# In the second attention VectorE opens each piece of the 4-bit codes at the end of the preceding step

## The chip, the cores and the metric

One core of a Trainium2 chip runs the whole program. The metric is device time in microseconds (us) from one launch to its end, the median over runs. The program holds two transformer layers; the change touches one stage of it, the second attention, in which TensorE (PE), VectorE (DVE), ScalarE (ACT), GpSimd (POOL) and the DMA queue of SyncE (SP) work side by side.

## The reference, cut to what matters

```python
# 4 x 256 tokens, width 512
x = layernorm(x + L0_attention(x)); x = layernorm(x + L0_gptq_ffn(x))
x = layernorm(x + L1_attention(x))          # 32 heads, 8 key heads, two causal attentions
x = layernorm(x + L1_nf4_ffn(x))
...
# in L1_nf4_ffn, for each of three weight matrices:
flat = w.reshape(-1, 64)
absmax = max(abs(flat), axis=1)
normalized = flat / where(absmax == 0, 1, absmax)
idx = searchsorted(bounds, normalized)      # 15 bounds, 16 codes
w = NF4_CODE[idx] * absmax
```

The code lookup is written as a sum of 15 steps: a first value plus, for every bound, a jump where `normalized` is at or above that bound. It depends on weights alone, so the kernel does it during the second attention and leaves the finished weights in DRAM for the last feed-forward block.

## The kernel before, in words

The second attention runs in 8 groups of 4 heads. A group has 16 steps (4 batches by 4 heads; each step handles two attentions of one head). `groups` (L1125) writes group 0 out, runs groups 1 to 6 as a loop of the engines (`Fori`), and writes group 7 out; so each engine takes the loop's branch back five times. No planner orders the work: each engine's order is the order of its own code, and semaphores tie the engines.

In step n VectorE does, in this order: `peaks(n)` (L1640, two reductions over the scores in PSUM, for which ScalarE's exponentials wait), `codes(n)`, `shares(n)` (L1646, reciprocals of the sums), `probs_low(n-1, 0)` (L1651, the low half of the turned probabilities of the first attention), `out_low(n-2)` (L1656), the rotation of one projected unit (L1619 to L1625), `probs_low(n-1, 1)` (L1651 again), in every fourth step `add_output` (L1664), and the step's remaining units, most of them the low half of a value unit (L1629, "the values") and in some steps a key unit (L1619 to L1625 at 256 columns).

ScalarE does in step n: `exps(n)` (L1348), `out_high(n-2)` (L1373), `probs_high(n-1, 0)` (L1367), `shares_applied(n)` (L1357), `code_terms(n)` (L1384, L1390), `probs_high(n-1, 1)` (L1367), then the high halves of the units (L1334, L1338). TensorE does `scores(n)`, a projection, `apply(n-2)`, `turn(n-1, 0)`, `output(n-3)`, `turn(n-1, 1)` (L1519, which waits for the first `probs_low`), then the remaining projections. GpSimd does in step n: splits of loaded weight pieces (L1260, L1262), the sums of the code terms (L1290), and the low half of the rotated unit (L1271), which the scores two steps later need.

The codes: a group handles 4 pieces of weights, 128 x 512 (the fourth 128 x 576). Each has 15 terms, spread over steps by `CODE_STEP`: the pieces begin in steps 0, 5, 8 and 11. About half of the terms of a step are VectorE's (L1710), the others ScalarE's, and GpSimd adds them up. A piece is opened by `code_start` on VectorE, four instructions: L1685 (largest magnitude by block of 64), L1688 and L1691 (its inverse, 8 or 9 columns), L1693 (the piece times the inverse, into `nf_unit`, which all terms read), each behind a wait for the one before; the last line is a wait of VectorE's queue for L1693 itself. A piece is closed by `code_end` (L1673, in place on the sum), which waits for GpSimd's last sum. In the kernel before, both stand in `codes(n)` of the piece's first step, behind `peaks(n)`: first `code_end` of the old piece, then `code_start` of the new one, then the first terms. SP's queue loads the next piece after `nf_unit_done` and stores a piece after `code_end`.

Of the kernel before, what the change touches and what calls it, by code (L numbers as in the profile page):

```python
# [22 lines left out]
GROUPS, PER = 8, 4  # L23
# [8 lines left out]
STEPS = PER * BATCH  # L32
# [973 lines left out]
def l1_units(first, last):  # L1006
# [7 lines left out]
CODE_AT = (0, 8 * BLK, 16 * BLK, 24 * BLK, 33 * BLK)  # L1014
CODE_STEP = [0] * 3 + [1] * 3 + [2] * 3 + [3] * 3 + [4] * 3 + [5] * 5 + [6] * 5 + [7] * 5 + [8] * 5 + [9] * 5 + [10] * 5 \
    + [11] * 3 + [12] * 2 + [13] * 2 + [14] * 4 + [15] * 4
CODE_RING = 5
STEEP = 2.0 ** 60

# [37 lines left out]
def l1_attention_block(nc, X, XT, LQ, signals, norm, normed, ident, banks, w_ql, w_vk, w_o, w_nf, coded_w, early):  # L1057

    NP = 2
    with ExitStack() as ctx:  # L1060
# [16 lines left out]
        nf_raw, nf_unit = sb("nf_raw", [P, LARGEST], F32), sb("nf_unit", [P, LARGEST], F32)  # L1077
        nf_acc, nf_term = sb("nf_acc", [P, CODE_AT[1] + LARGEST], F32), sb("nf_term", [P, CODE_RING, LARGEST], F32)
        lq_first = early["lq_w"]
# [82 lines left out]
        def code_slot_free(g, first, i):  # L1162

            if first and i < CODE_RING:
                return 0
            q, k = divmod(i - CODE_RING, 15)
            return 14 * (PER * g + q) + max(k, 1)

        def acc_cell(q, n):
            return nf_acc[:, q % 2 * CODE_AT[1]:q % 2 * CODE_AT[1] + n]  # L1170

        def code_cols(q):
            return CODE_AT[q], CODE_AT[q + 1] - CODE_AT[q]
# [59 lines left out]
        def _(pool):  # L1233
            def body(g, first, last):
# [39 lines left out]
                def code_sums(n):  # L1274

                    for i, step in enumerate(CODE_STEP):
# [6 lines left out]
                        acc = acc_cell(q, w)  # L1283
                        left = nf_term[:, (i - 1) % CODE_RING, 0:w] if k == 1 else acc
                        held = [(nf_terms_act, terms_made(g, i + 1, True)), (nf_terms, terms_made(g, i + 1, False)),
# [3 lines left out]
                        hold(pool, passed["pool"], *held)  # L1289
                        pool.tensor_tensor(acc, left, nf_term[:, i % CODE_RING, 0:w], ALU.add).then_inc(nf_added, 1)  # L1290

# [301 lines left out]
        def _(dve):  # L1593
# [10 lines left out]
            def body(g, first, last):  # L1604
                number, place = span("units", first, last, g)
                roped, roped_place = span("roped", first, last, g)
                plain, _ = span("plain", first, last, g)
# [24 lines left out]
                def unit_low(name):  # L1632
                    plain_low(name) if name[0] == "VL" else rotate(name)
# [33 lines left out]
                def code_end(q):  # L1667

                    _, n = code_cols(q % PER)
                    cell = acc_cell(q, n).rearrange("p (a c) -> p a c", c=BLK)  # L1670
                    wide = nf_top[:, q % 2, 0:n // BLK].unsqueeze(2).to_broadcast([P, n // BLK, BLK])
                    dve.wait_ge(nf_added, 14 * (PER * g + q + 1))
                    dve.scalar_tensor_tensor(out=cell, in0=cell, scalar=-1.0, in1=wide, op0=ALU.add, op1=ALU.mult)\  # L1673
                       .then_inc(nf_coded, 1)

                def code_start(q):

                    _, n = code_cols(q)
                    piece, m = PER * g + q, n // BLK
                    cut = lambda x: x[:, 0:n].rearrange("p (a c) -> p a c", c=BLK)  # L1680
                    top = nf_top[:, q % 2, 0:m]
                    dve.wait_ge(nf_landed, 16 * (piece + 1))
                    if not (first and q == 0):
                        dve.wait_ge(nf_terms_act, terms_made(g, 15 * q, True))
                    dve.tensor_reduce(top, cut(nf_raw), mybir.AxisListType.X, ALU.max, apply_absolute_value=True,  # L1685
                                      negate=True).then_inc(nf_measured, 1)
                    dve.wait_ge(nf_measured, 3 * piece + 1)
                    dve.scalar_tensor_tensor(out=nf_safe[:, 0:m], in0=top, scalar=0.0, in1=top, op0=ALU.is_equal,  # L1688
                                             op1=ALU.add).then_inc(nf_measured, 1)
                    dve.wait_ge(nf_measured, 3 * piece + 2)  # L1690
                    dve.reciprocal(nf_inv[:, 0:m], nf_safe[:, 0:m]).then_inc(nf_measured, 1)  # L1691
                    dve.wait_ge(nf_measured, 3 * piece + 3)
                    dve.tensor_tensor(cut(nf_unit), cut(nf_raw), nf_inv[:, 0:m].unsqueeze(2).to_broadcast([P, m, BLK]),  # L1693
                                      ALU.mult).then_inc(nf_unit_done, 1)
                    dve.wait_ge(nf_unit_done, piece + 1)

                def codes(n):
                    for q in range(PER):
                        ended = CODE_STEP[15 * q - 1] + 1 if q else 0
                        if ended == n and not (first and q == 0):  # L1700
                            code_end(q - 1)
                    for i, step in enumerate(CODE_STEP):
                        q, k = divmod(i, 15)
                        if step != n or CODE_ACT[i]:
                            continue
                        _, w = code_cols(q)
                        if k == 0:
                            code_start(q)
                        wait(dve, nf_added, code_slot_free(g, first, i))
                        dve.tensor_scalar(nf_term[:, i % CODE_RING, 0:w], nf_unit[:, 0:w], -BOUNDS[k], JUMPS[k],  # L1710
                                          ALU.is_ge, ALU.mult).then_inc(nf_terms, 1)
# [4 lines left out]
                for n in range(STEPS):  # L1716
                    peaks(n)
                    if first and n == 0:
                        normalise(dve, X, norm, 1, 1, late)
                    codes(n)  # L1720
                    shares(n)
                    if not (first and n < 1):
                        probs_low(n - 1, 0)
                    if not (first and n < 2):
                        out_low(n - 2)
                    units = l1_step_units(n, last)
                    for name in units[0:1]:
                        unit_low(name)
                    if not (first and n < 1):
                        probs_low(n - 1, 1)  # L1730
                    if n % PER == 2 and not (first and n < 3):
                        add_output(n - 3)
                        if last and n > PER:
                            tiles = range(2 * (n // PER) - 2, 2 * (n // PER))
                            dve.wait_ge(out_free, 2 * (BATCH * g + n // PER))
                            measure(dve, X, norm, normed, tiles)
                    for name in units[1:]:
                        unit_low(name)
                    if first and n < 2:
                        for i in range(2):  # L1740
                            low_tile(dve, XT, OUT[i], signals, 2, TT // 2 + 2 * n + i)
                    if first and n == 2:
                        lq_low(1, OUT[0])
# [558 lines left out]
```

## Time and profile before

| | |
|---|---|
| median of 3 runs | 2422.95 us (2421.2 to 2423.99) |
| profiled execution, its own time | 2422.93 us |
| its span | 2421.1 us, granted TensorE clock 0.971 |
| PE busy | 2239.8 us (93%) |
| DVE busy | 1804.6 us (75%) |
| ACT busy | 1433.2 us (59%) |
| POOL busy | 1577.2 us (65%) |
| second attention | about 786 to 2195 us of the span |

A row of the timeline is: start in us from the span's start, duration in us, engine, line, operation, tile written and tiles read (names as the program has them; tiles that share a buffer go by one name, so `q_packed` also stands for several small tiles, `q_hot` for the high halves of the probabilities), shapes, count of merged instructions, and in brackets the idle time of the engine before it with what ended it. A row with x2 or x3 merges back-to-back instructions. "issue" as a releaser means that the engine waited for nothing that the profile shows.

### The profile page before, as it was taken

To read this page: it belongs to the slowest core of one execution; us is meant where nothing else is said; L and a number is where in the kernel's file an instruction comes from. 1 tells how busy PE (TensorE), PEld (TensorE's weight loads), DVE (VectorE), ACT (ScalarE), POOL (GpSimd) and SP (SyncE) were. 2 spreads that over 40 slices of the span, in tenths; PEclk is the share of its full clock that TensorE was granted. 3 is DMA by queue.
4 is the path that set the end of the run, shared out by engine and by line. 5 is a ranking of instruction groups with operands and counts; after the bars stand their busy time and mean duration, and the time that the engine had idled before them with its cause. 6 is when DMAs were issued, how large, how long until landed. Compare 5 with 4: busy or idle time off the path is not lost. (4 is left out here: it accounts for less than half of the span.)

```text
span 2421.1 us, 43785 instructions
## 1 busy us (share of the span) xinstructions
PE 2239.8 (93%) x14144; PEld 1987.9 (82%) x14144; DVE 1804.6 (75%) x3266; ACT 1433.2 (59%) x3949; POOL 1577.2 (65%) x1340
## 2 busy tenths in 40 slices
PE   6899999988999899999999999999999999987998
PEld 5788888876888788888888888888888888876886
DVE  5788777767633898888888888888888888964332
ACT  2657766653233676676666666676676766663232
POOL 3656657413364678878878878788788788642343
PEclk8999999988999999999999999999999999988999
DMA  3201111000000101101101111111111111004000
GB/s 102 63 24 46 58 34 44 11 2 26 19 25 25 47 15 56 55 20 55 48 26 58 39 39 50 39 45 43 40 46 47 31 50 41 19 5 148 1 18 18
DMA packets 49556, 95.39 MB, mean 39 GB/s; under 512 B 6768, under 2 KB 14224, under 8 KB 48976
## 3 DMA queue, kind: packets, MB, share of 16 engines
q1 hardware_dynamic: 49296, 92.24, 12.2%
q8 instruction: 125, 2.05, 0.4%
q14 instruction: 135, 1.11, 0.1%
HBM read 81.47 MB, written 10.75 MB: 38 GB/s over the span
## 5 line engine op out<-in xcount | busy, mean ns | idle before, releaser
L1290 POOL TENSOR_TENSOR a_nf_acc<-a_nf_acc,a_nf_term 128x512 f32<-128x512 f32 (+1 forms) x416 | 588.9, 1416 | 145.4 <-ACT a_nf_term L1390 76.7
L1348 ACT ACTIVATE a_probs<-bank,q_packed 128x128 f32<-128x128 f32 (+1 forms) x512 | 208.4, 419 | 193.4 <-DVE q_packed L1640 193.4
L1357 ACT ACTIVATE a_probs<-a_probs,q_packed 128x128 f32<-128x128 f32 (+1 forms) x512 | 192.5, 463 | 68.9 <-DVE q_packed L1646 68.9
L1848 POOL TENSOR_TENSOR f_w_lo<-WGU,f_w_hi 128x512 fp32r<-128x512 f32 x88 | 112.4, 1295 | 175.5 <-ACT f_w_hi L1891 175.5
L1271 POOL TENSOR_TENSOR a_qk_lo<-q_packed,a_qk_hi 128x512 fp32r<-128x512 f32 (+1 forms) x160 | 193.7, 1212 | 44.5 <-ACT a_qk_hi L1334 44.5
L64 PE MATMUL bank<-a_wo_hi,a_ot_hi 128*128 128x512 f32 x512 | 212.5, 415 | 0.0
L1651 DVE TENSOR_TENSOR e_pt_lo<-bank,q_hot 128x384 fp32r<-128x384 f32 x256 | 141.0, 551 | 91.2 <-ACT q_hot L1367 90.4
L1710 DVE TENSOR_SCALAR a_nf_term<-a_nf_unit 128x512 f32<-128x512 f32 (+1 forms) x288 | 200.1, 740 | 3.4 <-DVE a_nf_unit L1693 0.9
L66 PE MATMUL bank<-a_wo_hi,a_ot_lo 128*128 128x512 f32 x512 | 201.4, 393 | 0.0
L65 PE MATMUL bank<-a_wo_lo,a_ot_hi 128*128 128x512 f32 x512 | 201.1, 393 | 0.0
L1334 ACT ACTIVATE a_qk_hi<-q_packed 128x512 fp32r<-128x512 f32 (+1 forms) x160 | 94.3, 590 | 176.0 <-DVE q_packed L1625 176.0
L480 ACT ACTIVATE a_probs<-bank,a_dip 128x128 f32<-128x128 f32 (+1 forms) x256 | 104.1, 419 | 139.5 <-DVE a_dip L903 139.5
L1519 PE MATMUL bank<-ident,a_probs 128*128 128x128 f32 x768 | 134.0, 284 | 56.5 <-DVE e_pt_lo L1651 56.5
L64 PE MATMUL bank<-q_hot,XT_hi 128*128 128x320 f32 x512 | 171.5, 335 | 6.9 <-DVE a_crossed L1622 6.9
L400 POOL TENSOR_TENSOR a_straight<-a_straight,a_crossed 128x512 f32<-128x512 f32 x64 | 82.1, 1283 | 132.2 <-DVE a_crossed L886 132.2
L1625 DVE TENSOR_TENSOR q_packed<-q_packed,a_crossed 128x512 f32<-128x512 f32 (+1 forms) x160 | 156.5, 978 | 5.5
L65 PE MATMUL bank<-q_table,XT_hi 128*128 128x320 f32 x512 | 160.2, 313 | 0.0
L1519 PEld LDWEIGHTS bank<-ident,a_probs 128*128 128x128 f32 x768 | 85.7, 142 | 90.7 <-DVE e_pt_lo L1651 82.2
L66 PE MATMUL bank<-q_hot,XT_lo 128*128 128x320 f32 x512 | 160.0, 313 | 0.0
L2028 DVE TENSOR_TENSOR f_hidden<-bank,f_act_gate 128x512 f32<-128x512 f32 x44 | 30.5, 692 | 165.9 <-PE bank L66 132.3
L64 PE MATMUL bank<-q_hot,a_vl_hi 128*128 128x256 f32 (+1 forms) x512 | 138.1, 270 | 9.0 <-DVE e_pt_lo L1651 8.4
L64 PE MATMUL bank<-XT_hi,f_w_hi 128*128 128x512 f32 x352 | 142.3, 404 | 3.2 <-POOL f_w_lo L1848 3.2
(244 smaller groups left out, 8461.1 us busy)
## 6 DMA issues: line engine op xcount, KB each, us to landing
q_packed<-in_l_o SPq DMA_DIRECT2D x64, 256.0 KB, 2.8
q_packed<-in_l_vk SPq DMA_DIRECT2D x32, 384.0 KB, 3.1
q_packed<-in_l_ql SPq DMA_DIRECT2D x32, 320.0 KB, 2.9
a_raw<-in_l_ou SPq DMA_DIRECT2D x32, 288.0 KB, 2.8
a_raw<-in_l_nr SPq DMA_DIRECT2D x16, 384.0 KB, 3.0
a_nf_raw<-in_w_nf SPq DMA_DIRECT2D x24, 256.0 KB, 2.6
coded_w<-a_nf_acc SPq DMA_DIRECT2D x24, 256.0 KB, 2.0
f_codes<-coded_w SPq DMA_DIRECT2D x6, 512.0 KB, 3.8
```

The source lines that it names most:

```text
L64: pe.matmul(out, lh, rh, start=first, stop=False)
L65: pe.matmul(out, lh, rl, start=False, stop=False)
L66: return pe.matmul(out, ll, rh, start=False, stop=last)
L1271: pool.tensor_tensor(rope_cell(name, QK.lo), src, rope_cell(name, QK.hi).bitcast(F32), ALU.subtract)\
L1290: pool.tensor_tensor(acc, left, nf_term[:, i % CODE_RING, 0:w], ALU.add).then_inc(nf_added, 1)
L1348: act.activation(probs[:, n % 2, col:col + keys], bank[:, at:at + keys], ACT.Exp, bias=dip[:, n % 2, i:i + 1], accum_out=total[:, n % 2, i ...
L1357: ins = act.activation(cell, cell, ACT.Copy, scale=share[:, n % 2, i:i + 1])
L1519: last_ = pe.transpose(TURN[:, i * P:(i + 1) * P], probs[:, n % 2, col:col + P], ident[:, :])
L1625: dve.tensor_tensor(row, row, crossed[:, 0:n], ALU.add).then_inc(rope_sum, 1)
L1651: dve.tensor_tensor(pt_lo_cell[:, at], TURN[:, 0:3 * P], pt_hi_cell[:, at].bitcast(F32), ALU.subtract)\
L1710: dve.tensor_scalar(nf_term[:, i % CODE_RING, 0:w], nf_unit[:, 0:w], -BOUNDS[k], JUMPS[k], ALU.is_ge, ALU.mult).then_inc(nf_terms, 1)
L1848: pool.tensor_tensor(lo, src, hi.bitcast(F32), ALU.subtract).then_inc(part_lo[i], 1)
```

## The change

`code_start` leaves `codes(n)`. A new function `next_code(n)` is called on VectorE at the end of step n, behind the remaining units. At the ends of steps 4, 7 and 10 it opens the group's second, third and fourth piece, and at the end of step 15 the first piece of the next group (except in the last group); only the very first piece is still opened in `codes(0)`. `code_end` stays in `codes` of steps 0, 5, 8 and 11, behind `peaks`. The instructions are the same ones, in another order on one engine; the other engines' code is unchanged. In `code_start` the piece's size is now taken modulo 4, as its number may be 4.

```diff
+CODE_STARTS = CODE_STEP[::15]
...
                 def code_start(q):
 
-                    _, n = code_cols(q)
+                    _, n = code_cols(q % PER)
...
+                def next_code(n):
+                    if n + 1 in CODE_STARTS:
+                        code_start(CODE_STARTS.index(n + 1))
+                    elif n == STEPS - 1 and not last:
+                        code_start(PER)
+
                 def codes(n):
-                    for q in range(PER):
-                        ended = CODE_STEP[15 * q - 1] + 1 if q else 0
-                        if ended == n and not (first and q == 0):
-                            code_end(q - 1)
+                    if n in CODE_STARTS and not (first and n == 0):
+                        code_end(CODE_STARTS.index(n) - 1)
                     for i, step in enumerate(CODE_STEP):
                         q, k = divmod(i, 15)
                         if step != n or CODE_ACT[i]:
                             continue
                         _, w = code_cols(q)
-                        if k == 0:
-                            code_start(q)
+                        if first and i == 0:
+                            code_start(0)
...
                     for name in units[1:]:
                         unit_low(name)
+                    next_code(n)
```

## Rows read from the trace of the kernel before

**Rows 1.** Waits of PE and DVE, 790 to 2196 us: total us, times, longest.
```profile
PE bank L1519 <- DVE e_pt_lo L1651: 56.5, 46, 4.9
DVE q_packed L1640 <- issue: 12.9, 5, 2.9
DVE q_packed L1640 <- PE bank L1508: 3.0, 9, 0.3
```

**Rows 2.** DVE timeline, step 6 of group 4, which opens no piece.
```profile
1549.49 1.01 DVE L1640 TENSOR_REDUCE q_packed<-bank 128x2 f32<-128x256 f32 x2
...
1553.15 0.56 DVE L1651 TENSOR_TENSOR e_pt_lo<-bank,q_hot 128x384 fp32r<-128x384 f32 x1 [0.69 <-ACT q_hot L1367]
...
1557.35 0.56 DVE L1651 TENSOR_TENSOR e_pt_lo<-bank,q_hot 128x384 fp32r<-128x384 f32 x1 [0.31 <-ACT q_hot L1367]
```

**Rows 3.** DVE timeline, step 5 of group 4, which opens the second piece.
```profile
1535.60 1.01 DVE L1640 TENSOR_REDUCE q_packed<-bank 128x2 f32<-128x256 f32 x2
1536.82 1.75 DVE L1673 SCALAR_TENSOR_TENSOR a_nf_acc<-a_nf_acc,q_packed 128x512 f32<-128x512 f32 x1 [0.21 <-POOL a_nf_acc L1290]
1538.49 0.68 DVE L1685 TENSOR_REDUCE q_packed<-a_nf_raw 128x8 f32<-128x512 f32 x1
...
1540.46 1.10 DVE L1710 TENSOR_SCALAR a_nf_term<-a_nf_unit 128x512 f32<-128x512 f32 x3
...
1541.57 0.53 DVE L1651 TENSOR_TENSOR e_pt_lo<-bank,q_hot 128x384 fp32r<-128x384 f32 x1
...
1546.04 0.56 DVE L1651 TENSOR_TENSOR e_pt_lo<-bank,q_hot 128x384 fp32r<-128x384 f32 x1 [0.63 <-ACT q_hot L1367]
```

**Rows 4.** POOL timeline of the same stretch.
```profile
1535.50 1.29 POOL L1290 TENSOR_TENSOR a_nf_acc<-a_nf_acc,a_nf_term 128x512 f32<-128x512 f32 x1 [0.18 <-POOL a_nf_acc L1290]
1536.75 1.27 POOL L1271 TENSOR_TENSOR a_qk_lo<-q_packed,a_qk_hi 128x512 fp32r<-128x512 f32 x1
```

**Rows 5.** Timelines of DVE and POOL, step 11 of group 4.
```profile
1604.43 1.56 DVE L1688 SCALAR_TENSOR_TENSOR q_packed<-q_packed 128x9 f32<-128x9 f32 x1
```
```profile
1604.40 1.56 POOL L1262 TENSOR_TENSOR a_wql_lo<-q_packed,a_wql_hi 128x640 fp32r<-128x640 f32 x1
```

**Rows 6.** Two lines of the source: count, shortest/median/longest ns, first and last start.
```profile
L1625 DVE TENSOR_TENSOR q_packed<-q_packed,a_crossed x160: 424/742/1857, 776.3 to 2153.2; 128x512 f32<-128x512 f32 x128, 128x256 f32<-128x256 f32 x32
```
```profile
L1693 DVE TENSOR_TENSOR a_nf_unit<-a_nf_raw,q_packed x32: 691/694/760, 791.0 to 2128.4; 128x512 f32<-128x512 f32 x24, 128x576 f32<-128x576 f32 x8
```

**Rows 7.** DVE and POOL timelines, step 8 of group 4, which opens the third piece.
```profile
1568.53 1.01 DVE L1640 TENSOR_REDUCE q_packed<-bank 128x2 f32<-128x256 f32 x2
...
1574.36 0.53 DVE L1651 TENSOR_TENSOR e_pt_lo<-bank,q_hot 128x384 fp32r<-128x384 f32 x1
```
```profile
1569.54 1.28 POOL L1271 TENSOR_TENSOR a_qk_lo<-q_packed,a_qk_hi 128x512 fp32r<-128x512 f32 x1
```

**Rows 8.** DVE timeline, step 11 of group 4, which opens the fourth piece.
```profile
1602.08 1.01 DVE L1640 TENSOR_REDUCE q_packed<-bank 128x2 f32<-128x256 f32 x2
...
1607.99 0.53 DVE L1651 TENSOR_TENSOR e_pt_lo<-bank,q_hot 128x384 fp32r<-128x384 f32 x1
```

**Rows 9.** DVE and POOL timelines where the loop branches back, groups 3 to 4.
```profile
1481.98 0.49 DVE L1629 TENSOR_TENSOR a_vl_lo<-bank,a_vl_hi 128x320 fp32r<-128x320 f32 x1 [0.56 <-ACT a_vl_hi L1338]
1485.02 1.02 DVE L1640 TENSOR_REDUCE q_packed<-bank 128x2 f32<-128x256 f32 x2 [2.55 <-issue]
...
1489.98 0.53 DVE L1651 TENSOR_TENSOR e_pt_lo<-bank,q_hot 128x384 fp32r<-128x384 f32 x1
```
```profile
1484.03 1.42 POOL L1290 TENSOR_TENSOR a_nf_acc<-a_nf_acc,a_nf_term 128x576 f32<-128x576 f32 x1 [0.18 <-POOL a_nf_acc L1290]
```

**Rows 10.** DVE timeline, step 0 of group 1, entered without a branch.
```profile
965.16 1.83 DVE L1673 SCALAR_TENSOR_TENSOR a_nf_acc<-a_nf_acc,q_packed 128x576 f32<-128x576 f32 x1 [2.06 <-POOL a_nf_acc L1290]
...
969.68 0.53 DVE L1651 TENSOR_TENSOR e_pt_lo<-bank,q_hot 128x384 fp32r<-128x384 f32 x1
```

**Rows 11.** DVE timeline, step 11 of group 7: L1673 at its shortest.
```profile
2126.60 0.68 DVE L1673 SCALAR_TENSOR_TENSOR a_nf_acc<-a_nf_acc,q_packed 128x512 f32<-128x512 f32 x1
```

## The prediction

> **What bounds the kernel now.** I read the waits of the second attention first, then the timelines of VectorE, GpSimd and ScalarE step by step, since the change only reorders one engine inside that stage.
>
> TensorE is the busiest engine, but it doesn't set the pace of this stage: it is the one that waits, 56.5 us in 46 places, for the low half of the first probabilities (L1651) [rows 1]. VectorE, in contrast, finds the scores ready when it comes to `peaks`: over 128 steps it waited 3.0 us in nine of them for PE, and 12.9 us in five for "issue" [rows 1]. So the pace is a ring of VectorE and ScalarE: peaks, then exponentials, `out_high` and `probs_high` on ScalarE, then `probs_low` on VectorE, and so on to the next peaks. An addition to this ring moves everything behind it, PE too.
>
> A step without an opening shows the ring at its fastest. From the start of peaks to the first L1651 it takes 1553.15 - 1549.49 = 3.66 us, and before that L1651 VectorE sat idle for ScalarE; from there to the second L1651 4.20 us, idle for ScalarE again [rows 2]. In a step that opens a piece VectorE is the late one: 1541.57 - 1535.60 = 5.97 us to the first L1651, with no idle before it, and 4.47 to the second, 10.44 in all [rows 3]. That is the stall the change aims at.
>
> **The change part by part.** Nothing is added or removed: four instructions and their waits go from behind peaks and `code_end` to ahead of peaks. The added waits of the queue are satisfied when reached: ScalarE made the terms of step n before `probs_high(n-1, 1)`, which VectorE has already waited for, and the load of the piece was issued a whole piece ago. SP's loads of the next piece are released some us earlier, its stores by `code_end` somewhat later; neither was late, cost nothing. ScalarE's terms aren't released earlier, as they stand behind `shares_applied`. GpSimd's first sum waits for VectorE's first two terms, which stay behind `code_end`.
>
> What moves is peaks. Call S the time from the opening's first instruction to peaks. After the change the first L1651 comes S + 3.66 after the end of the previous step, for the remaining work between (peaks 1.01, `code_end` 0.68 when undisturbed, three terms 1.10 [rows 3, 11]) is about 2.8 us and fits into ScalarE's 3.66. The second comes 4.20 later.
>
> How long is S? Alone, the opening takes 1540.46 - 1538.49 = 1.97 us [rows 3]. That is the lower end. But there it ran while GpSimd had nothing to do. At the end of a step GpSimd is adding terms and then makes the low half of the rotated unit: 1535.50 to 1536.79 and 1536.75 to 1538.02 [rows 4]. Some VectorE instructions don't run beside a GpSimd one: L1673 took 1.75 instead of 0.68 us [rows 3, 11] and ended 0.55 after GpSimd's instruction did [rows 3, 4]; L1688, a matter of 0.17 us, took 1.56 beside L1262, begun 0.03 earlier [rows 5]; L1625 goes from 424 to 1857 ns [rows 6]. L1693 was never longer than 760 [rows 6], but neither did it ever stand beside GpSimd work; it is the same operation as L1625, on two tiles in SBUF. I take it as held likewise. The upper end is then both L1688 and L1693 held for a whole GpSimd instruction of about 1.3 us: S = 4.5.
>
> The Trainium skill ("SBUF — State Buffer", section "SBUF: two separate sides") says that a VectorE instruction with two SBUF inputs and a GpSimd one that reads SBUF exclude each other, for the whole length of whichever began first. The rows of L1673 and L1688 agree; for L1693 no row here shows it, and the rule speaks for the held S, thus against this change. Without it one would take 1.97 for every opening.
>
> Step 5, worked through: L1685 runs 1535.60 to 1536.28; L1688 asks at 1536.31 and gets through when the sum ends at 1536.79; L1691 follows; L1693 asks at 1537.14 and must wait for GpSimd's L1271, now ending at 1538.06; it ends 0.55 later, at 1538.61; peaks start at 1538.70. S = 3.10. First L1651: 6.76 against 5.97. Second: 10.96 against 10.44, **+0.52**. The gain is real (the hold of L1673 and its 0.21 wait for GpSimd go, worth 1.28, since L1673 now runs when GpSimd is idle) but smaller than what replaces it: 1.13 of holds, and ScalarE's 3.66, no longer hidden under the opening.
>
> Step 8: GpSimd's L1271 ends at 1570.82 [rows 7], so L1693 ends near 1571.4 and S = 2.97; first L1651 at 6.63 against 5.83; second at 10.83 against 5.83 + 4.47 = 10.30: **+0.53**.
>
> Step 11: 5.91 us now [rows 8]; S lies between 2.1 (576 columns, not held) and 3.1. GpSimd works through L1271 and then the splits there, the place in the sequence is open, so I take 2.5: 6.16, **+0.25**.
>
> The loop's back edge, five times: here VectorE is idle 2.55 us ahead of peaks with nothing to wait for [rows 9]; five such places make the 12.9 us [rows 1]. It looks like a hole which the opening could fill. I don't think it does: the hole is the branch, and the branch stands behind `code_start`'s last line, the wait for L1693. So the sequence becomes opening, then branch, then peaks. L1685 from 1482.40; L1688 through at 1483.85, when a sum ends; L1693 held by the next sum (1484.03 to 1485.45) until 1486.04; then the branch. Between the start of the values' last instruction and peaks there are 1485.02 - 1481.98 = 3.04 us, between its end and peaks 2.55 [rows 9]; behind a wait I take 2.9. Peaks at 1488.95, first L1651 at 1492.61 instead of 1489.98: **+2.63** (2.3 to 2.8 by the two ends).
>
> The Trainium skill ("Runtime: NRT & Kernel Launch", section "Instruction fetch mechanics") says that a taken branch to a target outside the fetched window stalls until the page has come. The five idle stretches, one for each back edge, agree. By it nothing behind the branch can start earlier than the branch allows, and the opening's closing wait delays the branch.
>
> The two entries without a branch (groups 1 and 7): now 7.59 us from peaks (965.16 - 2.06 - 1.01 = 962.09) to 969.68, because `code_end` waited 2.06 for GpSimd and was held for 1.83 [rows 10]. After: held by two sums of 1.43 us, S = 3.9, plus 3.66 = 7.56: **0**.
>
> In group 7 step 11 L1673 isn't held now [rows 11], so the saving of 1.07 is missing from the balance: **+1.07**.
>
> Sum: 8 groups x (0.52 + 0.53 + 0.25) = 10.4; 5 x 2.63 = 13.2; 1.07; together +24.7 us. PE takes this over in full: its stall at `turn` grows by the same amounts, and it has no backlog to catch up with, since VectorE hardly ever waits for it. The profiled execution took 2422.93 us (span 2421.1 and 1.8 around it), the same as the median of 2422.95. 2422.9 + 24.7 = **2448 us**.
>
> **The rivals.**
>
> A. *The openings aren't held* (L1693 runs beside GpSimd, and L1688 slips through). Place: ends of steps 4, 7, 10, 15. For it: L1693's row has no long case. Against: L1625. With S = 1.97: step 5 9.83 against 10.44, -0.61; step 8 -0.47; step 11 -0.13: 8 x -1.21 = -9.7; back edge 1482.40 + 1.9 + 2.9 + 3.66 = 1490.9, +0.9 each, 4.6; the two entries, bound by GpSimd's sums, -1.8 each, -3.6; group 7 +1.1. Sum -7.6: **2415 us**, faster. It decides from a mean hold of 7.6 / 31 = 0.25 us for a moved opening; the forecast has about 1.0.
>
> B. *The branch hides the opening*, held as forecast: peaks at the back edge come when L1693 is done, 1486.1, first L1651 at 1489.8, -0.2 each. 10.4 + 1.1 - 1.0 = +10.5: **2433 us**. For it: the hole is there. Against: the wait ahead of the branch.
>
> C. *A and B together*: peaks at the back edge stay at 1485.02, first L1651 at 3.66 instead of 4.96, -1.3 each. -9.7 - 6.5 - 3.6 + 1.1 = -18.7: **2404 us**.
>
> D. *Holds and stalls are longer than forecast*: GpSimd gets through ahead of the waiting L1688 in a third of the 31 moved openings, 10 x 1.3 = 13, with PE's longer stalls costing it some clock: **2460 us**.
>
> E. *PE has slack that takes the additions up*, if its work had a reserve behind the stalls: the forecast is cut to under 5 us, **2426 us**. For it: in nine steps VectorE did wait for PE [rows 1]. Against it stands that PE waits for the same L1651 and moves along.
>
> **How the numbers follow.** Forecast 0.68, A 0.06, B 0.12, C 0.03, D 0.08, E 0.03. Range: B and the forecast and part of D: 2430 to 2457 us; A, C, E and the far part of D, under 2 in 10, are left out. The likeliest's own range is 2442 to 2453. A measurement of this kernel tells 0.2%, 4.8 us, from no change. Faster: A and C, 0.09. Same: E and a bit, 0.04. Slower 0.87.
>
> **What would show it.** L1693 at about 1.3 to 1.5 us in the changed trace where it was 0.69, and L1688 above 0.17 in several places; L1673 at 0.68 in steps 5 and 8. 6.6 to 6.8 us from the end of the values to the first L1651 in steps 5 and 8, with idle for ScalarE before it. At the back edge an idle stretch of 2.5 to 3.0 us behind L1693 and not before L1685, and PE's stall there some 2.6 us longer. PE's total wait for L1651 up from 56.5 to some 80. The prediction is wrong if L1693 stays at 0.69 (rival A) or if peaks follow L1693 without a hole at the back edge (rival B).

## The result, and the profile after

The changed kernel takes 2455.67 us (median of four runs, 2453.15 to 2458.24) against 2422.07 us of the kernel before beside it (four runs, 2421.1 to 2423.99): +33.6 us, ratio 1.0138 with a 95% interval of 1.0126 to 1.0151. The forecast was 2448 us, +25, with a range up to 2457. The sign and the mechanism hold; the size was short by about 9 us. The result also lies above the 2442 to 2453 us that the prediction gave its own case, and nearer to rival D's 2460 than to 2448.

In the changed kernel's listing the lines have moved: peaks L1641, the first-row reciprocal L1647, `probs_low` L1652, the rotation's last instruction L1626, `code_end` L1674, the opening L1686, L1689, L1692 and L1694, VectorE's terms L1715, GpSimd's sums L1291 and its low halves L1272.

From the page of the changed kernel, the engines' busy time and two groups of instructions (busy us, mean ns of one, idle before them and who ended it):

```profile
PE 2250.9 (92%) x14144; PEld 2001.4 (81%) x14144; DVE 1818.1 (74%) x3266; ACT 1429.9 (58%) x3949; POOL 1581.5 (64%) x1340
...
L1349 ACT ACTIVATE a_probs<-bank,q_packed 128x128 f32<-128x128 f32 (+1 forms) x512 | 208.8, 420 | 287.2 <-DVE q_packed L1641 287.2
...
L1358 ACT ACTIVATE a_probs<-a_probs,q_packed 128x128 f32<-128x128 f32 (+1 forms) x512 | 192.7, 469 | 6.8 <-DVE q_packed L1647 6.8
```

ScalarE's wait for the reciprocal (68.9 us before) is almost gone, because VectorE no longer comes to it late; its wait for peaks has grown from 193.4 to 287.2 us. What the change moved is in these two figures: VectorE is late for the first link of the ring instead of a later one. The waits of the changed kernel, 790 to 2232 us (total, times, longest), answer to [rows 1]:

```profile
PE bank L1520 <- DVE e_pt_lo L1652: 84.1, 47, 5.1
DVE q_packed L1641 <- issue: 15.7, 5, 3.3
DVE q_packed L1641 <- PE bank L1509: 1.9, 5, 0.8
```

TensorE waits 84.1 us for the first probabilities instead of 56.5, and the five idle stretches ahead of peaks are still there, and longer. VectorE at the end of step 4 and in step 5 of group 4, against [rows 3]:

```profile
1554.75 0.68 DVE L1686 TENSOR_REDUCE q_packed<-a_nf_raw 128x8 f32<-128x512 f32 x1
1555.46 0.51 DVE L1689 SCALAR_TENSOR_TENSOR q_packed<-q_packed 128x8 f32<-128x8 f32 x1
...
1556.24 1.49 DVE L1694 TENSOR_TENSOR a_nf_unit<-a_nf_raw,q_packed 128x512 f32<-128x512 f32 x1
1557.85 1.02 DVE L1641 TENSOR_REDUCE q_packed<-bank 128x2 f32<-128x256 f32 x2
1558.79 0.68 DVE L1674 SCALAR_TENSOR_TENSOR a_nf_acc<-a_nf_acc,q_packed 128x512 f32<-128x512 f32 x1
1559.39 1.09 DVE L1715 TENSOR_SCALAR a_nf_term<-a_nf_unit 128x512 f32<-128x512 f32 x3
...
1561.53 0.56 DVE L1652 TENSOR_TENSOR e_pt_lo<-bank,q_hot 128x384 fp32r<-128x384 f32 x1 [0.69 <-ACT q_hot L1368]
...
1565.72 0.56 DVE L1652 TENSOR_TENSOR e_pt_lo<-bank,q_hot 128x384 fp32r<-128x384 f32 x1 [0.31 <-ACT q_hot L1368]
...
1568.30 1.27 DVE L1626 TENSOR_TENSOR q_packed<-q_packed,a_crossed 128x256 f32<-128x256 f32 x1
1569.49 1.01 DVE L1641 TENSOR_REDUCE q_packed<-bank 128x2 f32<-128x256 f32 x2
```

GpSimd beside it:

```profile
1554.65 1.29 POOL L1291 TENSOR_TENSOR a_nf_acc<-a_nf_acc,a_nf_term 128x512 f32<-128x512 f32 x1 [0.18 <-POOL a_nf_acc L1291]
1555.90 1.28 POOL L1272 TENSOR_TENSOR a_qk_lo<-q_packed,a_qk_hi 128x512 fp32r<-128x512 f32 x1
...
1567.99 1.29 POOL L1272 TENSOR_TENSOR a_qk_lo<-q_packed,a_qk_hi 128x512 fp32r<-128x512 f32 x1
```

L1689 gets through when GpSimd's sum ends (1555.94), L1694 is held by the low half that begins at 1555.90 and ends 0.55 us after it (1557.73 against 1557.18). "Held" means here: the row is longer than the instruction takes alone, because it ends only after a GpSimd instruction that began before it. From L1686 to peaks are 1557.85 - 1554.75 = 3.10 us, and from peaks to the first L1652 3.68, with an idle for ScalarE in it. These are the forecast's 3.10 and 3.66.

The back edge, groups 4 to 5, VectorE, GpSimd and TensorE of the changed kernel:

```profile
1676.33 0.49 DVE L1630 TENSOR_TENSOR a_vl_lo<-bank,a_vl_hi 128x320 fp32r<-128x320 f32 x1 [0.56 <-ACT a_vl_hi L1339]
...
1677.44 0.79 DVE L1689 SCALAR_TENSOR_TENSOR q_packed<-q_packed 128x8 f32<-128x8 f32 x1
...
1678.50 1.85 DVE L1694 TENSOR_TENSOR a_nf_unit<-a_nf_raw,q_packed 128x512 f32<-128x512 f32 x1
1683.39 1.02 DVE L1641 TENSOR_REDUCE q_packed<-bank 128x2 f32<-128x256 f32 x2 [3.04 <-issue]
...
1687.06 0.56 DVE L1652 TENSOR_TENSOR e_pt_lo<-bank,q_hot 128x384 fp32r<-128x384 f32 x1 [0.69 <-ACT q_hot L1368]
```
```profile
1678.38 1.42 POOL L1291 TENSOR_TENSOR a_nf_acc<-a_nf_acc,a_nf_term 128x576 f32<-128x576 f32 x1 [0.18 <-POOL a_nf_acc L1291]
```
```profile
1687.68 0.90 PE L1520 MATMUL bank<-ident,a_probs 128*128 128x128 f32 x3 [4.84 <-DVE e_pt_lo L1652]
```

and the same place of TensorE in the kernel before:

```profile
1663.86 0.55 PE L1519 MATMUL bank<-ident,a_probs 128*128 128x128 f32 x3 [2.05 <-DVE e_pt_lo L1651]
```

The opening ends at 1680.35, and only then do three idle microseconds begin: the branch stands behind it. TensorE's stall is 2.79 us longer.

**Where the 33.6 us lie.** The starts of peaks, taken from both traces for all 128 steps, give the added time by place (changed minus before, us). 36.1 us come between the first and the last peaks; ahead of the stage and behind it the two profiled executions differ by -0.8. (The profiled execution of the changed kernel is the longest of its four, 2.6 us above the median, so this column adds up to more than 33.6.) The last column is the same difference for the pair e8 and e9 below.

| place | forecast | measured | e9 - e8 |
|---|---|---|---|
| steps 4 and 5, eight times | 4.2 | 7.1 | 4.3 |
| steps 6 to 9, eight times | 4.2 | 7.9 | 6.1 |
| steps 10 to 14, eight times | 3.1 | 0.8 | 0.9 |
| step 15 to step 3 over a back edge, five times | 13.2 | 18.3 | 21.6 |
| the same over the two entries | 0 | 1.9 | 0.1 |

### The profile page after: what moved, and what is told of

Same layout as the page of the kernel before. It is cut to its first block and busy times, and to the rows that moved or that the text cites. A ratio compares the mean times of both kernels' runs of the same rounds, so it can differ in the third digit from the quotient of the medians.

```text
span 2456.4 us, 43784 instructions
## 1 busy us (share of the span) xinstructions
PE 2250.9 (92%) x14144; PEld 2001.4 (81%) x14144; DVE 1818.1 (74%) x3266; ACT 1429.9 (58%) x3949; POOL 1581.5 (64%) x1340
## 3 DMA queue, kind: packets, MB, share of 16 engines
q8 instruction: 125, 2.05, 0.4%
## 5 line engine op out<-in xcount | busy, mean ns | idle before, releaser
L1291 POOL TENSOR_TENSOR a_nf_acc<-a_nf_acc,a_nf_term 128x512 f32<-128x512 f32 (+1 forms) x416 | 589.7, 1418 | 172.0 <-ACT a_nf_term L1391 108.5
L1349 ACT ACTIVATE a_probs<-bank,q_packed 128x128 f32<-128x128 f32 (+1 forms) x512 | 208.8, 420 | 287.2 <-DVE q_packed L1641 287.2
L1272 POOL TENSOR_TENSOR a_qk_lo<-q_packed,a_qk_hi 128x512 fp32r<-128x512 f32 (+1 forms) x160 | 198.2, 1240 | 56.9 <-ACT a_qk_hi L1335 56.9
L1652 DVE TENSOR_TENSOR e_pt_lo<-bank,q_hot 128x384 fp32r<-128x384 f32 x256 | 141.7, 553 | 109.5 <-ACT q_hot L1368 108.7
L1520 PE MATMUL bank<-ident,a_probs 128*128 128x128 f32 x768 | 136.3, 288 | 84.2 <-DVE e_pt_lo L1652 84.1
L1715 DVE TENSOR_SCALAR a_nf_term<-a_nf_unit 128x512 f32<-128x512 f32 (+1 forms) x288 | 202.2, 746 | 0.0
L1626 DVE TENSOR_TENSOR q_packed<-q_packed,a_crossed 128x512 f32<-128x512 f32 (+1 forms) x160 | 162.6, 1016 | 5.5
L1641 DVE TENSOR_REDUCE q_packed<-bank 128x2 f32<-128x256 f32 (+1 forms) x256 | 129.7, 547 | 20.5 <-issue 15.7
```

The source lines that it names most:

```text
L1272: pool.tensor_tensor(rope_cell(name, QK.lo), src, rope_cell(name, QK.hi).bitcast(F32), ALU.subtract)\
L1349: act.activation(probs[:, n % 2, col:col + keys], bank[:, at:at + keys], ACT.Exp, bias=dip[:, n % 2, i:i + 1], accum_out=total[:, n % 2, i ...
L1520: last_ = pe.transpose(TURN[:, i * P:(i + 1) * P], probs[:, n % 2, col:col + P], ident[:, :])
L1626: dve.tensor_tensor(row, row, crossed[:, 0:n], ALU.add).then_inc(rope_sum, 1)
L1641: ins = dve.tensor_reduce(dip[:, n % 2, 2 * r:2 * r + 2], scores, mybir.AxisListType.X, ALU.max, negate=True)
L1652: dve.tensor_tensor(pt_lo_cell[:, at], TURN[:, 0:3 * P], pt_hi_cell[:, at].bitcast(F32), ALU.subtract)\
```

## The experiments

Each kernel is compared with runs of the kernel before beside it on the same chip; their median was 2421.96 us for e1, e2, e3 and e6, 2422.01 for e4, e5 and e7, and 2421.39 for e8 and e9.

**e1: only the openings inside a group are moved.**

```
-                    elif n == STEPS - 1 and not last:
-                        code_start(PER)
...
-                        if first and i == 0:
+                        if i == 0:
                             code_start(0)
```

> Only the openings of the second to fourth piece are moved (ends of steps 4, 7, 10); a group's first piece is opened in step 0 as in the kernel before. My theory (ring of VectorE and ScalarE, openings held by GpSimd's instructions): +11 us by the sums of the prediction (8 x 1.3 + 1.1), +15 us with what the changed trace adds to the steps behind an opening (about 1.9 us in a group); 2434 to 2438 us. If the openings were not held: about -8 us, 2414 us. If only the loop's back edge costs anything: 0, 2422 us.

**e2: only the opening over the group's end is moved.**

```
-                    if n + 1 in CODE_STARTS:
-                        code_start(CODE_STARTS.index(n + 1))
-                    elif n == STEPS - 1 and not last:
+                    if n == STEPS - 1 and not last:
                         code_start(PER)
...
-                        if first and i == 0:
-                            code_start(0)
+                        if k == 0 and (q > 0 or first):
+                            code_start(q)
```

> Only the opening of the next group's first piece is moved (end of step 15); the others stay behind peaks and code_end. My theory (the loop's branch stands behind the opening's closing wait, and the opening is held): +13 us by the prediction, +18 us by the changed trace (5 x 3.2 at the back edges, 2 at the two entries without a branch); 2436 to 2441 us. If the branch's idle time hid the opening: -1 us, 2421 us. If this and the run with the inner openings are independent, the two differences add up to that of the whole change (+33.6 us).

Measured: e1 2440.15 us (ratio 1.0076, 1.0059 to 1.0093), +18.2; e2 2439.23 (1.0072, 1.0055 to 1.0089), +17.3. Together 35.5, near the 33.6 of the whole. So each half does its own harm, and the two add. Both are dearer than the forecast's terms, 11.5 and 13.2 us, and e1 lies above the 2434 to 2438 us expected of it.

**e3: the opening's closing wait stands ahead of the first term, so that the branch is not behind it.**

```
                                       ALU.mult).then_inc(nf_unit_done, 1)
-                    dve.wait_ge(nf_unit_done, piece + 1)
...
+                        if k == 0:
+                            dve.wait_ge(nf_unit_done, PER * g + q + 1)
```

> The whole change, but the last line of the opening, VectorE's wait for its own L1694, stands ahead of the piece's first term instead of at the opening's end. My theory: the branch can now be taken while L1694 is still held, so peaks at the five back edges come some 1.8 us earlier (L1694 took 1.85 us there), -9 us, and peaks after the other openings 0.1 to 0.2 us earlier, -3 us: about 2444 us, and the idle stretch between L1694 and peaks at the back edge shrinks from 3.0 to about 1.2 us. If the closing wait has no part in it (the branch is late for another reason): 2456 us, idle stretch unchanged at 3.0.

Measured: 2441.1 us (1.0076, 1.0059 to 1.0093), 14.6 below the changed kernel. VectorE's wait ahead of peaks, and TensorE's stall at the same back edge, in its trace:

```profile
DVE q_packed L1641 <- issue: 6.0, 5, 1.4
```
```profile
1680.27 0.90 PE L1520 MATMUL bank<-ident,a_probs 128*128 128x128 f32 x3 [3.01 <-DVE e_pt_lo L1652]
```

L1694 there still takes 1.84 us, but the idle behind it falls from 15.7 us in all to 6.0. So the branch does run beside the held instruction once nothing ahead of it waits for that instruction's end. Of the 18.3 us at the back edges 6.9 are left, and 9.7 of the 11.4 saved are this idle time: the wait in front of the branch, and not the opening itself, is most of that loss. It is rival B's mechanism, bought with one line; in the change as made it wasn't there.

**e6: the opening behind peaks, but ahead of `code_end`.**

```
-                    if n in CODE_STARTS and not (first and n == 0):
-                        code_end(CODE_STARTS.index(n) - 1)
+                    if n in CODE_STARTS:
+                        code_start(CODE_STARTS.index(n))
+                        if not (first and n == 0):
+                            code_end(CODE_STARTS.index(n) - 1)
...
-                    next_code(n)
```

> Each piece is opened in its first step as in the kernel before, behind peaks, but ahead of code_end instead of behind it. My theory: peaks stay early, so ScalarE's exponentials run beside the opening; the opening fills VectorE's wait for GpSimd's last sum, and only L1689 is held, by L1272, after which code_end runs free (0.68 us). First L1651 in steps 5 and 8 about 5.3 us behind the start of peaks instead of 5.97 and 5.83, at the back edge 4.4 instead of 5.0: 8 x 1.55 + 5 x 0.55 + 1.8 = -17 us, 2405 us. If the order of the same VectorE instructions behind peaks made no difference (the length of VectorE's work is what counts): 2422 us.

Measured: **2402.39 us** (ratio 0.9922, 0.9905 to 0.9938), 19.6 us below the kernel before and 53 below the changed one. It beats both. VectorE in its step 5 of group 4:

```profile
1525.81 1.01 DVE L1641 TENSOR_REDUCE q_packed<-bank 128x2 f32<-128x256 f32 x2
1526.74 0.68 DVE L1686 TENSOR_REDUCE q_packed<-a_nf_raw 128x8 f32<-128x512 f32 x1
1527.45 0.83 DVE L1689 SCALAR_TENSOR_TENSOR q_packed<-q_packed 128x8 f32<-128x8 f32 x1
...
1528.55 0.69 DVE L1694 TENSOR_TENSOR a_nf_unit<-a_nf_raw,q_packed 128x512 f32<-128x512 f32 x1
1529.38 0.69 DVE L1674 SCALAR_TENSOR_TENSOR a_nf_acc<-a_nf_acc,q_packed 128x512 f32<-128x512 f32 x1
...
1531.08 0.53 DVE L1652 TENSOR_TENSOR e_pt_lo<-bank,q_hot 128x384 fp32r<-128x384 f32 x1
```

The reduction L1686 takes its usual 0.68 beside GpSimd's low half (which runs from 1526.96), L1689 is held for 0.66, and by then GpSimd is done: L1694 and `code_end` run free. From peaks to the first L1652 are 5.27 us instead of 5.97 [rows 3]. It removes `code_end`'s hold, which the change aimed at, without putting anything ahead of peaks.

**e7: the opening right behind peaks, `code_end` at the end of the same step.**

```
-                    if n in CODE_STARTS and not (first and n == 0):
-                        code_end(CODE_STARTS.index(n) - 1)
+                    if n in CODE_STARTS:
+                        code_start(CODE_STARTS.index(n))
...
-                    next_code(n)
+                    if n in CODE_STARTS and not (first and n == 0):
+                        code_end(CODE_STARTS.index(n) - 1)
```

> Each piece is opened in its first step right behind peaks, and the old piece's code_end goes to the end of that step, behind the values, where the change had put the opening. My theory: the first L1651 comes 4.6 us behind the start of peaks in steps 5 and 8, but code_end then stands in the ring at the step's end, held by GpSimd's sums (0.7 to 1.9 us): gain of the one and loss of the other nearly cancel against the variant with the opening ahead of code_end: 2405 to 2418 us, 2411 us as the middle. If whatever stands at a step's end is free: 2400 us or less.

Measured: 2410.98 us (0.995, 0.9933 to 0.9966). The first L1652 comes 4.65 us behind peaks in step 5, earlier than in e6, but `code_end` at the end of the step is held in its turn (1.29 us in step 8, 1.59 in step 0) and stands ahead of the next peaks. So the end of a step is a bad place for `code_end` as well.

**e4 and e5: the kernels before and after, with GpSimd's sums in steps 4, 7, 10 and 15 cut to the first 64 columns (the other columns of these sums are left out).**

```
-                        pool.tensor_tensor(acc, left, nf_term[:, i % CODE_RING, 0:w], ALU.add).then_inc(nf_added, 1)
+                        w = BLK if n in (4, 7, 10, 15) else w
+                        pool.tensor_tensor(acc[:, 0:w], left[:, 0:w], nf_term[:, i % CODE_RING, 0:w], ALU.add)\
+                            .then_inc(nf_added, 1)
```

> The kernel before, in which GpSimd's sums of code terms in steps 4, 7, 10 and 15 cover only the first 64 of 512 or 576 columns; the other columns' additions are left out. So GpSimd is quiet at the ends of these steps. It is the control for the same cut in the changed kernel. My theory (VectorE's two-input instructions are held by GpSimd's): code_end is no longer held (saves 1.07, and its wait for the last sum), nor are L1625 and L1710 around it: -25 to -40 us, 2382 to 2397 us. If GpSimd's work were off VectorE's path: -2 us at most.

> The changed kernel with the same cut: GpSimd's sums in steps 4, 7, 10 and 15 cover only the first 64 columns; the other columns' additions are left out. My theory: the openings run free or nearly so, S falls from 3.1 to 2.0-2.2 us, L1694 takes 0.69 us again at the ends of steps 4 and 7; the whole falls by about 33 us or more from the changed kernel, to about 2415 to 2425 us, yet stays some 20 us slower than the control with the same cut, because peaks still stand behind the opening and the branch behind its wait. If the holds were the whole cause: equal to the control within 5 us. If they were no cause: the gap to the control stays at 33 us and L1694 at 1.5 us.

Measured: e4 2378.73 us (0.9827, 0.9811 to 0.9844), just below the 2382 to 2397 expected, and e5 2418.9 (0.9988, 0.9978 to 0.9997). L1694's counterpart in e5 (count; shortest/median/longest ns):

```profile
L1696 DVE TENSOR_TENSOR a_nf_unit<-a_nf_raw,q_packed x32: 691/693/759, 794.2 to 2125.8; 128x512 f32<-128x512 f32 x24, 128x576 f32<-128x576 f32 x8
```

against the changed kernel's:

```profile
L1694 DVE TENSOR_TENSOR a_nf_unit<-a_nf_raw,q_packed x32: 693/1485/1861, 791.2 to 2162.5; 128x512 f32<-128x512 f32 x24, 128x576 f32<-128x576 f32 x8
```

The hold of L1694 is gone from every opening, and the opening takes 1.96 us at steps 4 and 7. That shows GpSimd's work to be the cause of the hold. (In step 10 a short one is left: L1689's counterpart takes 0.99 us.) But the distance between the pair is 40.2 us and not about 20: I had expected the holds to be half of the loss, and this expectation fell. The control shows why. With GpSimd quiet at the step's end, `code_end` behind peaks isn't held either in steps 5 and 8 (0.68), and the first `probs_low` of step 5 comes at 4.60 us instead of 5.97. Against a ring of 3.68 there are then 0.92 us to gain, and an unheld opening of 1.96 ahead of peaks costs 1.04 (the two traces give 8.5 us for the eight places of steps 4 and 5, 1.06 each). A place's price is the opening's length less what the first `probs_low` can still gain down to ScalarE's 3.7 us. Holds enter both terms.

**e8 and e9: the kernels before and after, with GpSimd's sums of steps 0, 5 and 9 (from a piece's third term on) cut to 64 columns in the same way (the rest of those sums is left out).**

```
+                        w = BLK if n in (0, 5, 9) and k > 1 else w
```

> The kernel before, with GpSimd's sums of steps 0, 5 and 9 (from the third term of a piece on) cut to the first 64 columns; the other columns of these sums are left out. It is the control of the next run. Cutting takes short-lived GpSimd work from 64 of the places in which VectorE's step behind the openings can be held, so the control itself is 5 to 15 us faster than the kernel before: 2407 to 2417 us.

> The changed kernel with the same cut. The forecast was right up to the value it was worked out for (second probabilities of the step in steps 5 and 8, first ones at the back edge), and the changed kernel lost some 9 us more than forecast. Theory: those 9 us are instructions of VectorE further on (rotated units and terms of steps 0, 5 and 9), which now meet one of GpSimd's sums. Then this kernel is 22 to 29 us slower than its control, near the forecast's 24.7. Rival: the 9 us lie elsewhere (TensorE's longer stalls, its clock); then the distance to the control stays at 32 to 36 us, as it was between the two kernels in full.

Measured: e8 2407.83 us (0.9946, 0.9932 to 0.9959), e9 2444.77 (1.0092, 1.0076 to 1.0107): 36.9 us apart and not 22 to 29. So what GpSimd's sums hold isn't the whole of the missing 9 us. By place (the table's last column) it is a part: steps 4 and 5 drop from 7.1 to 4.3 us, which is the forecast's 4.2, and steps 6 to 9 from 7.9 to 6.1. At the back edges the loss grows instead, from 18.3 to 21.6. Where VectorE had been held, it now waits for TensorE, in step 1 of group 5 of e9:

```profile
1687.36 1.02 DVE L1643 TENSOR_REDUCE q_packed<-bank 128x2 f32<-128x256 f32 x2 [0.65 <-PE bank L1511]
...
1691.50 0.56 DVE L1654 TENSOR_TENSOR e_pt_lo<-bank,q_hot 128x384 fp32r<-128x384 f32 x1 [1.16 <-ACT q_hot L1370]
```

Stretches of e9 behind its stall of 4.96 us (the stretch, its length, busy us and instructions of PE, PE's weight loads, DVE, ACT and POOL, then the granted clock, and the DMA engines' share and GB/s):

```profile
1682.00:1684.00 2.00, 2.00 (x10) 2.00 (x9) 1.97 (x4) 1.97 (x4) 0.06 (x1) 0.50 0.03 11
1684.00:1686.00 2.00, 2.00 (x10) 2.00 (x9) 1.30 (x3) 0.96 (x3) 0.65 (x2) 0.50 0.04 8
```

TensorE runs at 0.50 of its clock, the 1.2 GHz level, through some 4 us of solid work, and the next scores come late.

## Why the prediction came out as it did

**What bounds the stage: right.** The ring of VectorE and ScalarE sets the pace. The two halves of the change, moved alone, add up, and in steps 0, 5, 8 and 11 of the groups above the first `probs_low` follows peaks by 3.68 us, ScalarE's chain.

**The length S of the opening: right.** Forecast 3.10, 2.97, 2.5 us, 3.9 for the entries. Peaks of steps 5, 8 and 11 came 3.10, 2.97 and 2.52 us later in the middle groups, those behind the entries 3.82. L1694 was held by GpSimd as L1625 had been, which no row of the kernel before showed; the Trainium skill ("SBUF — State Buffer", section "SBUF: two separate sides") had it so, and L1694's median of 1.49 us agrees, as does its 0.69 in e5 where GpSimd is brief.

**The gain from `code_end`: right.** 0.68 us in steps 5 and 8 where it took 1.75; no wait for GpSimd's last sum ahead of it.

**Up to the second `probs_low` of steps 5 and 8: right.** 3.10 + 7.87 = 10.97 us forecast 10.96, and 2.96 + 7.87 = 10.83 forecast 10.83. At the back edge the first `probs_low` is 1687.06 - 1676.33 = 10.73 us behind the start of the values' last instruction, and was 1489.98 - 1481.98 = 8.00 [rows 9]: +2.73, forecast +2.63.

**The branch behind the opening: right, and a little dearer.** The five idle stretches make 15.7 us, 3.14 each, where I had taken 2.9. The cause I gave, the closing wait ahead of the branch, is shown by e3. Over the five back edges the first `probs_low` comes 14.2 us later instead of 13.2.

**What failed: the tacit step that nothing changes behind the point to which a place was worked out.** "The second comes 4.20 later", and with it each place was closed, the back edges even at the first `probs_low`. This put at nothing what comes behind.

First and largest, VectorE meets other GpSimd instructions in the rest of the step. In step 5 L1626 takes 1.27 us, as it now asks 0.31 us behind the start of a low half (1568.30, 1567.99); before it asked later and paid 0.95. The same rows of the kernel before, VectorE and GpSimd:

```profile
1548.61 0.95 DVE L1625 TENSOR_TENSOR q_packed<-q_packed,a_crossed 128x256 f32<-128x256 f32 x1
```
```profile
1547.99 1.29 POOL L1271 TENSOR_TENSOR a_qk_lo<-q_packed,a_qk_hi 128x512 fp32r<-128x512 f32 x1
```

That is +0.32, on top of the forecast +0.52: 0.84 of the measured 0.89 a place. In step 9 the terms are held, VectorE and GpSimd of the changed kernel

```profile
1601.54 3.28 DVE L1715 TENSOR_SCALAR a_nf_term<-a_nf_unit 128x512 f32<-128x512 f32 x3
...
1604.83 0.52 DVE L1652 TENSOR_TENSOR e_pt_lo<-bank,q_hot 128x384 fp32r<-128x384 f32 x1
```
```profile
1601.62 1.48 POOL L1272 TENSOR_TENSOR a_qk_lo<-q_packed,a_qk_hi 128x512 fp32r<-128x512 f32 x1
1603.06 1.48 POOL L1291 TENSOR_TENSOR a_nf_acc<-a_nf_acc,a_nf_term 128x512 f32<-128x512 f32 x1
```

and in the kernel before

```profile
1581.01 2.03 DVE L1710 TENSOR_SCALAR a_nf_term<-a_nf_unit 128x512 f32<-128x512 f32 x3
```

Three terms meet two GpSimd instructions in a row and last 3.28 us instead of 2.03; the first `probs_low` comes at 4.22 us and no longer at 3.67. Both are borne out by e8 and e9 for steps 4 to 9, where cutting the sums took off 2.8 and 1.8 us of the surplus.

Behind a back edge it is the rotation's last instruction. VectorE and GpSimd in step 0 of group 5 of the changed kernel, and VectorE of the kernel before:

```profile
1690.25 1.59 DVE L1626 TENSOR_TENSOR q_packed<-q_packed,a_crossed 128x512 f32<-128x512 f32 x1
```
```profile
1690.02 1.28 POOL L1291 TENSOR_TENSOR a_nf_acc<-a_nf_acc,a_nf_term 128x512 f32<-128x512 f32 x1 [2.66 <-ACT a_nf_term L1391]
```
```profile
1666.44 0.69 DVE L1625 TENSOR_TENSOR q_packed<-q_packed,a_crossed 128x512 f32<-128x512 f32 x1
```

Because the opening is gone from behind peaks, L1626 now asks 0.23 us after a sum has begun. From the first `probs_low` to the second it takes 4.70 to 4.73 us in step 0 of groups 2 to 6, where it took 3.77: 4.7 us in all, nearly the whole 5.1 by which the back edges exceed the forecast. In e9, which cuts that sum, it takes 3.80. (The rest: 1.1 us from the longer idle at the branch, and 0.6 given back in step 1.)

Second, after most back edges TensorE comes out of its stall at the lower clock, here out of one of 4.84 us. The changed kernel behind 1687:

```profile
1687.00:1689.00 2.00, 1.32 (x6) 1.32 (x7) 1.92 (x4) 2.00 (x6) 0.36 (x1) 0.60 0.44 130
1689.00:1691.00 2.00, 2.00 (x10) 2.00 (x9) 1.95 (x3) 1.11 (x3) 0.98 (x1) 0.55 0.00 0
```

and the kernel before, behind its stall of 2.05:

```profile
1665.00:1667.00 2.00, 2.00 (x15) 1.90 (x15) 1.94 (x3) 1.60 (x3) 0.49 (x1) 1.00 0.00 0
```

Over the stage the same 8508 matmuls keep TensorE busy 12.2 us longer (changed kernel, then the one before):

```profile
790.00:2196.00 1406.00, 1292.16 (x8508) 1173.50 (x8508) 1189.49 (x2027) 923.90 (x2556) 1081.82 (x839) 0.98 0.12 39
```
```profile
790.00:2160.00 1370.00, 1279.94 (x8508) 1159.49 (x8509) 1175.97 (x2027) 928.05 (x2555) 1078.71 (x839) 0.99 0.13 40
```

"PE takes this over in full: its stall at `turn` grows by the same amounts" failed by this: the stalls grew by 27.6 us where peaks moved by 36.1, while TensorE's own work took 12.2 us more. The clock was in rival D as an aside, without a price. But most of these 12.2 us filled time in which TensorE would have waited. VectorE's waits for it ahead of peaks fell, from 3.0 us to 1.9. At the back edge from group 2 to 3 the stall was 2.83 us and the granted clock behind it stayed at 1.00:

```profile
1330.00:1332.00 2.00, 1.82 (x13) 1.83 (x14) 1.99 (x4) 1.97 (x5) 0.00 (x0) 1.00 0.25 95
```

That edge cost 3.16 us, and the four at the lower clock 3.50, 3.65, 3.24 and 4.76. Only the last, behind a stall of 5.05 us, stands out: there VectorE waited 0.42 us for the scores of step 1. From these five I estimate that the clock cost the back edges one to two us in the changed kernel. e9 shows that it stands right behind the hold: take the hold away and VectorE waits for TensorE instead, so curing the hold alone wins nothing there. No kernel was run that keeps the clock up through the stall.

Third, one term was too high, and by the same mechanism. Steps 10 to 14 cost 0.8 us and not 3.1. In the middle groups L1626 takes 1.84 us in step 11 where it took 0.69, then 0.69 in step 12 where it took 1.86, and 1.53 in step 13 where it took 1.00: a hold left step 12 and others came. By peaks the group loses 0.6 us in steps 10 and 11, wins 1.1 in 12 and loses 0.5 in 13. No experiment singles this out. The entries, forecast at 0, are at 0 up to the first `probs_low` (-0.1 and 0.0) and cost 1.9 behind it; in e2, which has the same opening there, they cost -0.1, so this isn't the opening's doing alone, and its cause stays open.

**The rivals.** A (openings not held) gave 2415 us, and a kernel almost without holds at the step's end, e5, took 2418.9; but its own control took 2378.7, so A's arithmetic of a gain held only as long as `code_end` alone was counted as held. B (the branch hides the opening) comes true in e3, where the closing wait is moved: 2441.1 against B's 2433. C did not arise. D's extra holds of L1689, its main term, did not come (0.37 us median, 0.79 at the longest), its clock did. That the time is near D's is thus mostly chance: what made it longer is mainly holds further on in the step, which no rival named. E is refuted: TensorE's idle grew with VectorE's lateness.

## What to carry to other kernels

Work moved to the end of a step is ahead of the next step's first link, and it is free only if that link was not the one that everybody waits for. Price such a move by where it stands after, including what the neighbour engine runs there, and try the place behind the link first: here it was worth 19.6 us, against a loss of 33.6. Don't leave a wait for one's own last instruction ahead of a loop's branch; put it where the result is used. And follow a shift past the point where the local sum closes, at least to the next instruction that shares something with another engine.

## What the runs showed of the hardware

A closing wait in front of a loop's branch made VectorE idle 3.0 to 3.3 us behind the held instruction; with the wait behind the branch 1.1 to 1.4 us were left. In the kernel before, where nothing was held ahead of the branch, it was 2.45 to 2.9 us. The idle is thus not a fixed price but a latency that a running instruction can cover. The Trainium skill ("Runtime: NRT & Kernel Launch", section "Instruction fetch mechanics") says that a taken branch out of the fetched window waits for its page. An idle stretch at each of the five back edges agrees, though no row shows the fetch itself; e3 adds that the instruction already running goes on meanwhile.

A term with a single input in SBUF (L1715, 0.41 us alone) is held beside GpSimd as well. The Trainium skill (the SBUF section named above) counts a VectorE instruction in a 2-port perf mode among those that take the port pair shared with GpSimd, and the 512 columns in 0.41 us, against 0.68 for `code_end`, fit such a mode. The holds go both ways: in these stretches GpSimd's L1272 takes 1.48 us instead of 1.28. It takes an instruction of only 128 x 8 elements to meet one: L1689, 0.17 us alone, took 0.79 at the back edges.

TensorE's granted clock stayed at 1.00 behind a stall of 2.05 us and fell to 0.60 and 0.55 in the two stretches behind one of 4.84. In between the stall's length alone does not tell. In e3 it was at the 1.2 GHz level behind a stall of 3.01 us:

```profile
1681.00:1683.00 2.00, 2.00 (x9) 2.00 (x9) 1.94 (x4) 1.70 (x3) 0.40 (x1) 0.50 0.00 0
```

but it stayed at 1.00 behind one of 2.90 in the same kernel and of 2.83 in the changed one, and in the kernel before it fell behind a stall of 1.88 us that ended at 1368.87:

```profile
1370.00:1372.00 2.00, 2.00 (x9) 2.00 (x9) 1.94 (x4) 2.00 (x4) 0.98 (x2) 0.50 0.00 0
```
